# Local attention layers: turning the softmax weights in the two row halves of the array, with the odd heads' token halves of v swapped

## The chip, the cores and the metric

One core of a Trainium2 chip runs the whole program. The metric is the device time of one execution in microseconds (us). The engines are named as in the profile: PE (TensorE, with its weight loads as PEld), DVE (VectorE), ACT (ScalarE), POOL (GpSimd) and SP (the queue that issues DMAs).

## The reference

The program computes four residual blocks over x of shape (8, 512, 256), each followed by a layer norm: a 16-head attention with a gate, a slot attention with 16 experts, a retention block, and two local attention layers. The change touches the last block alone. Cut to what matters, one of its two layers is

```
h = shift_token(x); q, k, v = split(h @ wqkv)            # 8 heads of 64
q, k = rotary_xpos(l2norm(q) * qs, l2norm(k) * ksc)
# blocks of 128 queries; each looks at its own 128 keys and the 128 before
sim = where((i < j) | (i > j + 128) | (j == -1), -max, q * 8 @ k.T)
o = softmax(sim) @ v
x = x + o @ wo
h = layer_norm(shift_token(x)) @ w1 + b1
x = x + (a * gelu(g)) @ w2 + b2                          # a, g = split(h)
```

The first block of each sequence has no keys before it (the mask j == -1).

## The kernel before

All engines follow orders written out by hand and meet at semaphores (`wait_ge`, `then_inc`); `Fresh.wait_ge` (L40) leaves out waits already seen. Blocks 1 to 3 of the program end at about 1000 us; what follows is `Block4`.

**Slots.** Block 4 works on 64 tiles (2 layers x 8 sequences x 4 blocks of 128 tokens). `tensor4`, `scalar4`, `vector4` and `gpsimd4` (L1872, L2082, L2188, L2388) walk through slots n = 1, 2, ... and in each treat four tiles at different stages: a = n (projection), b = n - 1 (turning q and k, scores, exp), c = n - 2 (dividing by the sums, turning the weights), d = n - 3 (attend, output projection, adding to x). The MLP of a sequence is spread in pieces over four parts of each slot (`mlp_pieces`, L1786), and repeats every four slots.

PE's order in a slot is: queries' projection (L1932), turn q (L1958), keys' projection, turn k, MLP part 1, attend d (L2011 for a tile that opens a sequence, L2017 and L2022 for others), scores b (L1976), values a (L1946), MLP part 2, turn half of c's weights (L1991), output projection d (L2033), turn the other half, MLP parts 3 and 4. In the MLP, L2073 and L2077 are the gate and lin products, L2051 the product down, L2059 and L2064 turn x and the normalised rows.

**Turning the weights.** The softmax weights of a head have queries on partitions, but attend needs keys there. `tensor4_weights` (L1980) turns them by 128x128 blocks with the identity as the moving operand: per pair of heads 2 heads x 2 windows (the keys before, the own keys), or 2 x 1 for an opening tile. Each pair fills one bank. DVE copies the banks of pairs 0 and 2 (`vector4_weights`, L2305, L2311), ACT those of 1 and 3 (`scalar4_weights`, L2158, L2164). The divided weights stand in `probs[i % 2]`, where max, exp and divide also work.

**Attend.** `tensor4_attend` (L1994) runs in four quadrants of the array: a 64-row half of the keys by a 64-column head. Sums over the two row halves go to banks 5 and 2; because of the mask, half of each window's block is zero and is left out. ACT copies bank 2 (L2105), DVE adds bank 5 (`vector4_sums`, L2266, L2269). An opening tile uses all 128 rows and bank 5 alone, and DVE copies it (L2274).

**The ring of banks.** Banks 3, 4, 6, 7 are a ring (`Ring`, L60). The list of its uses in `layout4` (L1823) follows PE's order: q, k, part 1's pieces, the four score banks, part 2's pieces, the four banks of turned weights, parts 3 and 4. Before PE writes a bank, `emptied4` (L1859) waits until the use four places earlier has been emptied: scores by DVE's max (L2258), q by ACT (`scalar4_queries`, L2130, L2134), k by DVE's copy (L2202), a gate by ACT's GELU (L2184), a lin by DVE (L2351), back and hT by DVE and ACT (L2343, L2175, L2347, L2179), down by DVE (L2334).

**DVE, ACT, POOL.** DVE in a slot: divide c (L2240, L2244), copy k, squared lengths a (L2281), MLP part 1, sums d, max b, MLP part 2, copy weights 0, rotate a's queries (L2292, L2295), add d to x (L2225), copy weights 2, rotate a's keys, MLP part 3, scale a (`vector4_scale`, L2303), MLP part 4. In slots with n mod 4 = 3, part 4 also takes row statistics (L2616, L2619), and part 1 of the slot after ends with a normalise of four operations (L2631). ACT: divide c (L2127), copy q, squares a (L2141), MLP part 1, copy bank 2, copy values (L2147), exp b, first half (L2155), MLP part 2, copy weights 1, exp second half, copy weights 3, parts 3 and 4. POOL: `gpsimd4_tile` (L2398) takes the power -1/2 of the lengths (L2407) and adds the halves of the rotation (L2411); `gpsimd4_mlp` copies rows and adds a bias (L2431, L2439).

```
for group in range(2):
    for hh in range(2):
        self.emptied4(w, "s", i, 2 * group + hh)
```

is how scores take two banks at a time.

## Time and profile before

| | us |
|---|---|
| three runs | 2330.47, 2332.06, 2335.05 (median 2332.06) |
| the profiled execution | 2333.25 |
| its span, first to last instruction | 2331.4 |
| mean granted clock of PE | 0.989 |

In the rows, a line of the timeline is: start in us from the span's start, length in us, engine, line of the kernel, operation, operands, count, and in brackets the idle time before it with what ended it. A matmul's end is modelled and overlaps the next one's start, so starts are read. The compiler makes two MATMUL instructions of each f32 product and one of each turned block, and the counts are counts of instructions.

### The profile page before, as it was taken

The page shows a single profiled execution, that of the slowest core. Times are in us where ns is not written, and L with a number is a line of the kernel's source. Part 1 is how long each engine was busy: PE and PEld are TensorE (multiplying, and loading weights), DVE is VectorE, ACT ScalarE, POOL GpSimd, SP SyncE. Part 2 cuts the span into 40 slices and gives each one's busy share as a digit, 9 for nine tenths or more (in the row PEclk, how much of TensorE's full clock was granted, in tenths as well). Part 3 has the DMA queues.
Part 4 walks back from the last instruction along what each step waited for, and adds up shares of the span by engine and source line. Part 5 has one row for each costly group of instructions (what it writes and reads, how often), then busy time and mean ns, then how long its engine had stood idle before and what let it go on. Part 6 is the DMA issues. An engine that isn't in the chain of part 4 may idle for free.

```text
span 2331.4 us, 42446 instructions
## 1 busy us (share of the span) xinstructions
PE 2239.6 (96%) x16257; PEld 1316.2 (56%) x16306; DVE 1635.1 (70%) x4252; ACT 1254.6 (54%) x2823; POOL 732.4 (31%) x730
## 2 busy tenths in 40 slices
PE   7999999999998999989899999999999999999998
PEld 3333333334634867756566666666666666666665
DVE  6788888886502746668777677677767777787763
ACT  4666666665222622247666656665665665566640
POOL 3344323321111411144433233333333333333321
PEclk7999999999998999999999999999999999999999
DMA  7454343333397020010000000000001000000001
GB/s 240 151 158 121 117 119 122 112 91 109 157 422 297 2 91 19 28 39 3 5 6 6 5 2 6 6 2 32 15 6 53 6 15 24 19 6 24 22 23 40
DMA packets 68617, 158.44 MB, mean 68 GB/s; under 512 B 6256, under 2 KB 49120, under 8 KB 63936
## 3 DMA queue, kind: packets, MB, share of 16 engines
q1 hardware_dynamic: 65856, 146.55, 17.8%
q0 software_dynamic: 2560, 9.18, 1.7%
q8 instruction: 130, 2.13, 0.4%
q14 instruction: 71, 0.58, 0.1%
HBM read 116.39 MB, written 35.13 MB: 65 GB/s over the span
## 4 chain that ended last, share of the span: by engine, by line
PE 73%; DVE 14%; DMA 4%; ACT 4%; issue 3%; POOL 1%; SPq 0%; another core or an unknown queue 0%; POOLq 0%; DVEq 0%; ACTq 0%
PE banks L2073 10%; PE banks L2051 7%; PE banks L1932 6%; PE banks L1946 5%; PE banks L232 4%; PE banks L274 4%; PE banks L2033 3%; PE banks L245 3%; PE banks L1976 3%; PE banks L1991 3%; DMA arena<-in_e_W 3%; DVE arena L483 2%; PE banks L1455 2%; PE banks L1958 2%; PE banks L300 2%
## 5 line engine op out<-in xcount | busy, mean ns | idle before, releaser
L483 DVE TENSOR_REDUCE arena<-banks 128x1 f32<-128x512 f32 x512 | 322.6, 681 | 61.2 <-PE banks L232 60.4
L395 ACT ACTIVATE arena<-banks 128x512 f32<-128x512 f32 x512 | 280.3, 596 | 136.1 <-PE banks L245 112.4
L2073 PE MATMUL banks<-arena 128*128 128x512 f32 x640 | 293.2, 594 | 1.0 <-DVE arena L2258 1.0
L2155 ACT ACTIVATE arena<-arena 128x256 f32<-128x256 f32 (+1 forms) x512 | 286.5, 562 | 5.0 <-DVE arena L2264 4.5
L2411 POOL TENSOR_TENSOR arena<-arena 128x512 f32<-128x512 f32 x128 | 162.8, 1272 | 379.8 <-DVE arena L2295 379.8
L1932 PE MATMUL banks<-arena 128*128 128x512 f32 x512 | 241.5, 594 | 2.8 <-DVE arena L2295 2.8
L232 PE MATMUL banks<-arena 96*128 96x512 bf16 x512 | 202.9, 400 | 14.6 <-DVE arena L483 8.9
L2407 POOL TENSOR_TENSOR arena<-arena 128x16 f32<-128x16 f32 x64 | 189.4, 2959 | 5.4
L2127 ACT ACTIVATE arena<-arena 128x256 f32<-128x256 f32 (+1 forms) x256 | 102.1, 471 | 162.9 <-DVE arena L2240 162.9
L2073 PEld LDWEIGHTS banks<-arena 128*128 128x128 f32 x640 | 115.5, 190 | 126.7 <-issue 116.5
L245 PE MATMUL banks<-arena 128*128 128x512 bf16 x463 | 174.6, 382 | 3.1 <-ACT arena L395 2.2
L2051 PE MATMUL banks<-arena 128*128 128x256 f32 x768 | 171.1, 379 | 1.9 <-DVE arena L2351 1.9
L2258 DVE CUSTOM_DVE_ANT_0 arena<-banks,arena 128x256 f32<-128x256 f32 (+1 forms) x512 | 168.7, 386 | 3.5 <-PE banks L1976 3.5
L2051 PEld LDWEIGHTS banks<-arena 128*128 128x128 f32 x768 | 144.5, 190 | 28.0 <-issue 6.2
L232 PEld LDWEIGHTS banks<-arena 96*128 96x128 bf16 x512 | 50.0, 98 | 181.5 <-DVE arena L483 110.9
L1932 PEld LDWEIGHTS banks<-arena 128*128 128x128 f32 x512 | 91.5, 190 | 86.9 <-issue 81.3
L274 PE MATMUL banks<-arena 128*32 128x512 f32 x1024 | 136.4, 605 | 2.5 <-ACT arena L395 1.6
L2147 ACT ACTIVATE arena<-banks 128x512 f32<-128x512 f32 x64 | 38.2, 597 | 180.4 <-PE banks L1946 180.4
L2303 DVE TENSOR_TENSOR arena<-arena 128x512 f32<-128x512 f32 x64 | 81.9, 1279 | 73.6 <-POOL arena L2411 73.6
L1946 PE MATMUL banks<-arena 128*128 128x512 f32 x256 | 126.7, 617 | 0.3 <-ACT arena L2105 0.3
L2033 PE MATMUL banks<-arena 128*128 128x256 f32 x512 | 121.2, 380 | 0.0
L1991 PE MATMUL banks<-arena 128*128 128x128 f32 x896 | 119.8, 272 | 0.5 <-DVE arena L2258 0.3
(304 smaller groups left out, 4225.7 us busy)
## 6 DMA issues: line engine op xcount, KB each, us to landing
arena<-in_e_W SPq DMA_DIRECT2D x16, 2048.0 KB, 15.6
arena<-stacks SPq DMA_DIRECT2D x64, 384.0 KB, 4.7
arena<-in_e_Wg SPq DMA_DIRECT2D x8, 2048.0 KB, 17.6
stacks<-arena SPq DMA_DIRECT2D x32, 384.0 KB, 2.5
stacks<-arena SPq DMA_DIRECT2D x32, 256.0 KB, 2.8
arena<-dens POOLq DMA_DIRECT2D x32, 256.0 KB, 4.8
arena<-in_xT SPq DMA_DIRECT2D x8, 512.0 KB, 7.8
stacks<-arena SPq DMA_DIRECT2D x32, 128.0 KB, 2.6
```

Source lines behind the costliest of these rows:

```text
L232: e.matmul(self.psum[:, k % 3], stack[0:STACK, 0, j, t * P:(t + 1) * P], stack[0:STACK, 1, j, :], start=True, stop=True).then_inc(s["a_max ...
L245: e.matmul(self.psum[:, self.exp_bank1(k)], stack[:, 1, j, t * P:(t + 1) * P], stack[:, 0, j, :], start=True, stop=True).then_inc(s["a_exp ...
L274: i = e.matmul(bank[32 * j:32 * j + 32, :], v[:, t, at:at + 32], ex[:, j], start=t == 0, stop=t == TILES - 1, skip_group_check=True)
L395: e.activation(ex[:, j], self.psum[:, self.exp_bank1(k)], ACT.Exp).then_inc(s["a_e"], 1)
L483: e.tensor_reduce(split(self.maxima[n % 2][:, 0:16], TILES, UNIT)[:, t, j:j + 1], self.psum[:, k % 3], AX.X, ALU.max, negate=True).then_in ...
L1932: k = e.matmul(self.psum[:, side], self.xT[:, b, c, at:at + P], self.wqkv4[:, c, side], start=c == 0, stop=c == 1)
L1946: k = e.matmul(self.psum[:, 2], self.xT[:, b, c, at:at + P], self.wqkv4[:, c, 2], start=c == 0, stop=c == 1)
L1991: k = e.transpose(bank[:, hh, n], pr[:, 2 * pair + hh, n * P:(n + 1) * P], self.ident)
L2033: k = e.matmul(self.psum[:, 2, 0:CH], self.o4[0][:, pair * P:(pair + 1) * P], self.wo4[:, pair], start=pair == 0, stop=pair == 3)
L2051: i = e.matmul(bank[:, t % 2 * CH:(t % 2 + 1) * CH], self.hidden[k][:, at:at + P], self.w2[:, k + t // 2 if last else k], start=k == 0, st ...
L2073: i = e.matmul(bank, weights[:, c], self.hT[:, c], start=c == 0, stop=c == 1)
L2155: k = e.activation(pr[:, h, at:], pr[:, h, at:], ACT.Exp, bias=mx[:, h:h + 1], scale=rn[:, h:h + 1], accum_out=den[:, h:h + 1])
```

## The change

- The turning of c's weights moves from parts 2 and 3 to just after MLP part 1, ahead of attend, on PE; the copies of the turned weights move on ACT and DVE to just after their MLP part 1, ahead of bank 2's copy and of the sums. The ring's list of uses moves with it.
- `probs[0]` now holds scores and exps of every tile; the divide writes into `probs[1]` in another arrangement (`probs4`), where each head pair's eight half windows lie such that three 128-column pairs of half blocks hold what the mask leaves. Turning takes, per head pair, three pairs of instructions, one in each 64-row half of the array, each with 128 weight columns and 64 moving columns, into two banks (two pairs for an opening tile). A `couple` is two head pairs, and waits for both of its banks.
- The copies take 384 columns per bank instead of 512, DVE the banks of the first row half, ACT those of the second. `pT` becomes two sets, used in turn.
- Odd heads thus find their keys in swapped 64-token halves. So `tensor4_values` makes their values from `swapped`, a copy of the tokens with halves exchanged, made by POOL (`gpsimd4_swap`, four copies of 128x64 per tile, ahead of the tile's other POOL work), in four products of 256 columns instead of two of 512.
- `tensor4_attend` reads the new arrangement; an opening tile now also runs in quadrants, so ACT's copy of bank 2 and DVE's add are done for all tiles.

The core of the diff:

```diff
-        self.pT = [split(r.take(512), 2, 2, P) for _ in range(4)]
+        self.pT = [[split(r.take(768), 2, 2, 192) for _ in range(2)] for _ in range(2)]
+        self.swapped = [split(r.take(256), CHUNKS, P) for _ in range(2)]
...
+                if part == 1 and 0 <= c < TILES4:
+                    uses += [("w", c, index) for index in range(4)]
                 if part == 1 and 0 <= b < TILES4:
                     uses += [("s", b, index) for index in range(4)]
-                if part == 2 and 0 <= c < TILES4:
-                    uses += [("w", c, index) for index in range(4)]
...
     def tensor4(self, e, w):
...
+            if c is not None:
+                self.tensor4_weights(e, w, c, 0)
+                self.tensor4_weights(e, w, c, 1)
             if d is not None:
                 self.tensor4_attend(e, w, d)
...
-                self.tensor4_weights(e, w, c, 0)
-                self.tensor4_weights(e, w, c, 1)
             if d is not None:
                 self.tensor4_out(e, w, d)
-            if c is not None:
-                self.tensor4_weights(e, w, c, 2)
-                self.tensor4_weights(e, w, c, 3)
...
     def tensor4_values(self, e, w, i):
...
-        if i >= 3 and (i - 3) % TILES:
-            w.wait_ge("t_oa", halves_before(i - 3) + 1)
-        for c in range(CHUNKS):
-            at = 1 - c + t * P
-            k = e.matmul(self.psum[:, 2], self.xT[:, b, c, at:at + P], self.wqkv4[:, c, 2], start=c == 0, stop=c == 1)
+        if i >= 3:
+            w.wait_ge("t_oa", i - 2)
+        w.wait_ge("t_swap", i + 1)
+        out = split(self.psum[:, 2], PAIRS, 2, HD4)
+        for hh in range(2):
+            for c in range(CHUNKS):
+                at = 1 - c + t * P
+                tokens = self.swapped[i % 2][:, c] if hh else self.xT[:, b, c, at:at + P]
+                k = e.matmul(out[:, :, hh], tokens, split(self.wqkv4[:, c, 2], PAIRS, 2, HD4)[:, :, hh], start=c == 0, stop=c == 1, skip_group_check=True)
...
-    def tensor4_weights(self, e, w, i, pair):
-        windows = (0, 1) if i % TILES else (1,)
-        bank = split(self.bank4("w", i, pair), 2, 2, P)
-        pr = split(self.probs[i % 2][:, 0:2048], H4, 2 * P)
-        if pair % 2:
-            w.wait_ge("t_pna", 2 * i + pair // 2 + 1)
-        else:
-            w.wait_ge("t_pn", 2 * i + pair // 2 + 1)
-        self.emptied4(w, "w", i, pair)
-        for hh in range(2):
-            for n in windows:
-                k = e.transpose(bank[:, hh, n], pr[:, 2 * pair + hh, n * P:(n + 1) * P], self.ident)
-        k.then_inc(self.s["t_pT"], 1)
+    def probs4(self, i, h):
+
+        pair, hh = divmod(h, 2)
+        raw = split(self.probs[0][:, 0:2048], H4, 2, 2, 64)[:, h]
+        view = split(self.probs[1][:, 512 * pair:512 * pair + 512], 2, 4, 64)
+        view = view[:, :, 1:3] if hh else view[:, :, 0::3]
+        return (raw, view) if i % TILES else (raw[:, 1:], view[:, 1:])
+
+    def tensor4_weights(self, e, w, i, couple):
+        banks = [self.bank4("w", i, 2 * couple + half) for half in range(2)]
+        w.wait_ge("t_pn", 2 * i + couple + 1)
+        w.wait_ge("t_pna", 2 * i + couple + 1)
+        self.emptied4(w, "w", i, 2 * couple)
+        self.emptied4(w, "w", i, 2 * couple + 1)
+        places = [(0, 0, 1), (1, 1, 2), (2, 2, 3)] if i % TILES else [(3, 1, 0), (2, 2, 1)]
+        for n in range(2):
+            for place in places:
+                last = n == 1 and place == places[-1]
+                for half in range(2):
+                    if i % TILES:
+                        source, to = place[0] + half, place[0]
+                    else:
+                        source, to = place[0], place[1 + half]
+                    rows, at = slice(64 * half, 64 * half + 64), 512 * (2 * couple + n) + P * source
+                    k = e.transpose(banks[half][:, 192 * n + 64 * to:192 * n + 64 * to + 64], self.probs[1][rows, at:at + P], self.ident[rows, rows])
+                    if last:
+                        k.then_inc(self.s["t_pT"], 1)
...
     def tensor4_attend(self, e, w, i):
...
+            outer, inner = split(pT, 3, 2, 64)[:, 1:3, 0], split(pT, 3, 2, 64)[:, 0:2, 1]
+            for hh in range(2):
+                cols = slice((2 * pair + hh) * HD4, (2 * pair + hh + 1) * HD4)
+                for half in range(2):
+                    rows = slice(64 * half, 64 * half + 64)
+                    near = half == hh
+                    v = own if near or i % TILES == 0 else ahead
+                    k = e.matmul(self.psum[64 * hh:64 * hh + 64, 2 if half else 5, pair * P:(pair + 1) * P], v[rows, cols], outer[rows] if near else inner[rows],
+                                 start=True, stop=i % TILES == 0, skip_group_check=True)
...
     def scalar4(self, e, w):
...
+            self.scalar4_mlp(e, w, n, 1)
+            if c is not None:
+                self.scalar4_weights(e, w, c, 0)
+                self.scalar4_weights(e, w, c, 1)
+            if n == 2:
                 self.scalar3_turn(e, w, SEQS - 1, 0)
-            self.scalar4_mlp(e, w, n, 1)
-            if d is not None and d % TILES:
+            if d is not None:
...
-                self.scalar4_weights(e, w, c, 1)
             if b is not None:
                 self.scalar4_exp(e, w, b, 1)
-            if c is not None:
-                self.scalar4_weights(e, w, c, 3)
...
     def scalar4_divide(self, e, w, i):
...
+        if i:
+            w.wait_ge("t_pT", 4 * i)
         for pair in (1, 3):
             for h in (2 * pair, 2 * pair + 1):
-                k = e.activation(pr[:, h, at:], pr[:, h, at:], ACT.Copy, scale=rden[:, h:h + 1])
+                raw, turned = self.probs4(i, h)
+                k = e.activation(turned, raw, ACT.Copy, scale=rden[:, h:h + 1])
...
     def vector4(self, e, w):
...
             self.vector4_mlp(e, w, n, 1)
+            if c is not None:
+                self.vector4_weights(e, w, c, 0)
+                self.vector4_weights(e, w, c, 1)
             if d is not None:
                 self.vector4_sums(e, w, d)
...
-                self.vector4_weights(e, w, c, 0)
...
-                self.vector4_weights(e, w, c, 2)
...
     def vector4_max(self, e, w, i, half):
...
+        pr, mx = split(self.probs[0][:, 0:2048], H4, 2 * P), self.probs[i % 2][:, 2048:2056]
+        if i:
+            w.wait_ge("t_pn", 2 * i)
+            w.wait_ge("t_pna", 2 * i)
...
     def vector4_sums(self, e, w, i):
...
-        if i % TILES:
-            w.wait_ge("t_oa", halves_before(i) + 1)
-            k = e.tensor_tensor(self.o4[0], self.o4[0], self.psum[:, 5], ALU.add)
-        else:
-            w.wait_ge("t_av", i + 1)
-            if i:
-                w.wait_ge("t_wo", i)
-            k = e.tensor_copy(self.o4[0], self.psum[:, 5])
-        k.then_inc(self.s["t_o"], 1)
+        w.wait_ge("t_oa", i + 1)
+        e.tensor_tensor(self.o4[0], self.o4[0], self.psum[:, 5], ALU.add).then_inc(self.s["t_o"], 1)
...
     def vector4_weights(self, e, w, i, couple):
...
+        to, bank = self.pT[i % 2][couple][:, :, 0], split(self.bank4("w", i, 2 * couple)[:, 0:384], 2, 192)
+        at = 0 if i % TILES else 64
+        w.wait_ge("t_pT", 4 * i + 2 * couple + 1)
+        if i >= 2:
+            w.wait_ge("t_av", i - 1)
+        e.tensor_copy(to[:, :, at:], bank[:, :, at:]).then_inc(self.s["t_pTd"], 1)
...
     def gpsimd4(self, e, w):
...
+                self.gpsimd4_swap(e, w, n)
                 self.gpsimd4_tile(e, w, n)
             self.gpsimd4_mlp(e, w, n)
+
+    def gpsimd4_swap(self, e, w, n):
+        l, b, t = n // LAYER, n // TILES % SEQS, n % TILES
+        if l:
+            w.wait_ge("m_yTd", b + 1)
+            w.wait_ge("m_yTa", b + 1)
+        else:
+            w.wait_ge("r_xTb", b + 1)
+            w.wait_ge("r_xTa", b + 1)
+        if n >= 2:
+            w.wait_ge("t_v", n - 1)
+        for c in range(CHUNKS):
+            at = 1 - c + t * P
+            e.tensor_copy(self.swapped[n % 2][:, c, 0:64], self.xT[:, b, c, at + 64:at + P])
+            k = e.tensor_copy(self.swapped[n % 2][:, c, 64:P], self.xT[:, b, c, at:at + 64])
+        k.then_inc(self.s["t_swap"], 1)
```

## Rows read from the trace of the kernel before

**Rows 1.** The page, part 1: PE's busy time, share of the span, instructions.

```profile
PE 2239.6 (96%) x16257; PEld 1316.2 (56%) x16306; DVE 1635.1 (70%) x4252; ACT 1254.6 (54%) x2823; POOL 732.4 (31%) x730
```

**Rows 2.** Windows: stretch, length, busy time of each engine, granted clock, DMA.

```profile
1000.00:1170.00 170.00, 150.82 (x1368) 98.11 (x1362) 133.33 (x430) 105.56 (x282) 75.58 (x68) 0.99 0.05 16
...
1200.00:2220.00 1020.00, 1017.85 (x7920) 668.51 (x7921) 750.81 (x2237) 616.89 (x1516) 359.66 (x278) 1.00 0.05 14
...
1653.06:1671.27 18.21, 18.21 (x114) 11.10 (x112) 13.28 (x40) 12.99 (x31) 6.10 (x6) 1.00 0.05 14
1671.27:1693.00 21.73, 21.56 (x185) 15.22 (x184) 19.33 (x54) 10.87 (x28) 9.63 (x8) 1.00 0.00 1
...
1713.70:1733.08 19.38, 19.38 (x158) 11.66 (x157) 12.32 (x40) 13.21 (x32) 5.72 (x4) 1.00 0.01 3
sum 80.02, PE 79.85 PEld 52.53 DVE 57.32 ACT 48.47 POOL 27.32; mean PE 19.96 PEld 13.13 DVE 14.33 ACT 12.12 POOL 6.83
```

**Rows 3.** Timeline of PE in slot A: a turned group and what follows.

```profile
1664.35 1.04 PE L1991 MATMUL banks<-arena 128*128 128x128 f32 x8
1665.23 1.89 PE L2033 MATMUL banks<-arena 128*128 128x256 f32 x8
```

**Rows 4.** Groups by line and form: turning, its loads, and ordinary loads.

```profile
L1991 PE MATMUL banks<-arena 128*128 128x128 f32 x896 | 119.8, 272 | 0.5 <-DVE arena L2258 0.3
...
L2051 PEld LDWEIGHTS banks<-arena 128*128 128x128 f32 x768 | 144.5, 190 | 28.0 <-issue 6.2 <-DVE arena L2351 3.5
...
L1991 PEld LDWEIGHTS banks<-arena 128*128 128x128 f32 x896 | 105.0, 140 | 23.3 <-issue 15.3
```

**Rows 5.** Timeline of PE in block 2: four row tiles, 32 moving columns.

```profile
743.70 1.99 PE L990 MATMUL banks<-arena 32*128 32x32 f32 x64 [0.60 <-DVE arena L1217]
```

**Rows 6.** Timeline of PE in slot A: attend, scores, values.

```profile
1658.38 1.04 PE L2011 MATMUL banks<-arena 128*64 128x128 f32 x16
1659.35 1.53 PE L1976 MATMUL banks<-arena 64*64 64x192 f32 x32
1660.81 1.98 PE L1946 MATMUL banks<-arena 128*128 128x512 f32 x4
```

**Rows 7.** Timeline of PE in slot D: attend's start, scores, values.

```profile
1719.82 0.45 PE L2017 MATMUL banks<-arena 64*64 64x128 f32 x8
...
1721.21 1.48 PE L1976 MATMUL banks<-arena 64*64 64x192 f32 x32
1722.62 1.98 PE L1946 MATMUL banks<-arena 128*128 128x512 f32 x4
```

**Rows 8.** DVE's scale multiply, all 64: shortest, median, longest in ns.

```profile
L2303 DVE TENSOR_TENSOR arena<-arena x64: 687/693/2832, 1021.6 to 2226.8; 128x512 f32<-128x512 f32 x64
```

**Rows 9.** Timeline of ACT in A, B and D: gate 5, queries' copy, gate 2.

```profile
1658.60 0.47 ACT L2184 ACTIVATE arena<-banks,arena 128x256 f32<-128x256 f32 x1 [0.64 <-PE banks L2077]
...
1676.27 0.57 ACT L2134 ACTIVATE arena<-banks 128x512 f32<-128x512 f32 x1
...
1719.93 0.69 ACT L2184 ACTIVATE arena<-banks,arena 128x512 f32<-128x512 f32 x1 [1.56 <-PE banks L2073]
```

**Rows 10.** Timeline of DVE from A's end into B: scale, lin 5, normalise.

```profile
1670.93 1.21 DVE L2303 TENSOR_TENSOR arena<-arena 128x512 f32<-128x512 f32 x1 [0.43 <-POOL arena L2411]
...
1678.55 0.48 DVE L2351 SCALAR_TENSOR_TENSOR arena<-banks,arena 128x256 f32<-128x256 f32 x1
1678.94 1.37 DVE L2631 TENSOR_SCALAR arena<-arena 128x256 f32<-128x256 f32 x4
```

**Rows 11.** Timeline of PE in slot B: scores' second half, values.

```profile
1679.08 0.88 PE L1976 MATMUL banks<-arena 64*64 64x192 f32 x16 [0.17 <-DVE arena L2351]
1679.89 1.98 PE L1946 MATMUL banks<-arena 128*128 128x512 f32 x4
```

**Rows 12.** Timeline of DVE in slot C: the keys' copy.

```profile
1697.52 0.69 DVE L2202 COPY arena<-banks 128x512 f32<-128x512 f32 x1 [1.94 <-PE banks L1958]
```

**Rows 13.** Timeline of PE in slot C: scores, values.

```profile
1698.80 1.06 PE L1976 MATMUL banks<-arena 64*64 64x64 f32 x32
1699.79 1.98 PE L1946 MATMUL banks<-arena 128*128 128x512 f32 x4
```

More of the change, by code:

```diff
@@ L1994, in tensor4_attend @@
     def tensor4_attend(self, e, w, i):
-        first = i % TILES == 0
-        w.wait_ge("t_vn", i + 1)
+        w.wait_ge("t_vn", min(i + 3, TILES4))
         if i:
             w.wait_ge("t_o", i)
-        if not first:
             w.wait_ge("t_x", i)
+        own, ahead = self.vn[i % 4], self.vn[(i - 1) % 4]
         for pair in range(PAIRS):
-            if pair % 2:
-                w.wait_ge("t_pTa", 2 * i + pair // 2 + 1)
-            else:
-                w.wait_ge("t_pTd", 2 * i + pair // 2 + 1)
-            heads = [slice((2 * pair + hh) * HD4, (2 * pair + hh + 1) * HD4) for hh in range(2)]
-            if first:
-                for hh in range(2):
-                    k = e.matmul(self.psum[64 * hh:64 * hh + 64, 5, pair * P:(pair + 1) * P], self.vn[i % 4][:, heads[hh]], self.pT[pair][:, hh, 1],
-                                 start=True, stop=True, skip_group_check=True)
+            w.wait_ge("t_pTd", 2 * i + pair // 2 + 1)
+            w.wait_ge("t_pTa", 2 * i + pair // 2 + 1)
+            pT = self.pT[i % 2][pair // 2][:, pair % 2].rearrange("p a b -> p (a b)")
+            outer, inner = split(pT, 3, 2, 64)[:, 1:3, 0], split(pT, 3, 2, 64)[:, 0:2, 1]
[7 more added lines that the diff above has]
+                                 start=True, stop=i % TILES == 0, skip_group_check=True)
+            if i % TILES == 0:
@@ L2013, in tensor4_attend @@
                 continue
             for hh in range(2):
-                for half, (bank, n) in enumerate(((5, 1), (2, 0))):
+                cols = slice((2 * pair + hh) * HD4, (2 * pair + hh + 1) * HD4)
+                for half in range(2):
                     rows = slice(64 * half, 64 * half + 64)
-                    k = e.matmul(self.psum[64 * hh:64 * hh + 64, bank, pair * P:(pair + 1) * P], self.vn[(i - 1 + n) % 4][rows, heads[hh]], self.pT[pair][rows, hh, n],
-                                 start=True, stop=False, skip_group_check=True)
@@ L2019, in tensor4_attend @@
-            for hh in range(2):
-                for half, (bank, n) in enumerate(((5, 0), (2, 1))):
-                    rows, some = slice(64 * half, 64 * half + 64), slice(64 * half, 64 * half + 64)
-                    k = e.matmul(self.psum[64 * hh:64 * hh + 64, bank, pair * P + 64 * half:pair * P + 64 * half + 64], self.vn[(i - 1 + n) % 4][rows, heads[hh]],
-                                 self.pT[pair][rows, hh, n, some], start=False, stop=True, skip_group_check=True)
+                    near = half == hh
@@ L2024, in tensor4_attend @@
+                    at = 0 if near else 64
+                    k = e.matmul(self.psum[64 * hh:64 * hh + 64, 2 if half else 5, pair * P + at:pair * P + at + 64], (ahead if near else own)[rows, cols],
+                                 pT[rows, 0:64] if near else pT[rows, 320:384], start=False, stop=True, skip_group_check=True)
         k.then_inc(self.s["t_av"], 1)
@@ L2156, in scalar4_exp, with scalar4_weights @@
         k.then_inc(self.s["t_exp"], 1)
-    def scalar4_weights(self, e, w, i, pair):
-        b4 = split(self.bank4("w", i, pair), 2, 2, P)
-        at = 0 if i % TILES else 1
-        w.wait_ge("t_pT", 4 * i + pair + 1)
-        if i:
-            w.wait_ge("t_av", i)
-        e.activation(self.pT[pair][:, :, at:], b4[:, :, at:], ACT.Copy).then_inc(self.s["t_pTa"], 1)
+    def scalar4_weights(self, e, w, i, couple):
+        to, bank = self.pT[i % 2][couple][:, :, 1], split(self.bank4("w", i, 2 * couple + 1)[:, 0:384], 2, 192)
+        end = 192 if i % TILES else P
+        w.wait_ge("t_pT", 4 * i + 2 * couple + 2)
+        if i >= 2:
+            w.wait_ge("t_av", i - 1)
+        e.activation(to[:, :, 0:end], bank[:, :, 0:end], ACT.Copy).then_inc(self.s["t_pTa"], 1)
     def scalar4_mlp(self, e, w, slot, part):
@@ L2235, in vector4_divide @@
     def vector4_divide(self, e, w, i):
-        at = 0 if i % TILES else P
-        pr, extra = split(self.probs[i % 2][:, 0:2048], H4, 2 * P), self.probs[i % 2][:, 2048:]
+        extra = self.probs[i % 2][:, 2048:]
         den, rden = extra[:, 8:16], extra[:, 16:24]
```

33 lines of the change are left out of this document (11 added, 22 removed).

## The prediction, made before any run of the changed kernel

> **What bounds the kernel now.** I read the page first, then windows, then one engine at a time. The page's busy times [rows 1] only say that TensorE (PE) is the fullest engine over the whole span; the windows say where. From 1200 to 2220 us, inside the local layers, PE is busy 1017.85 of 1020 us at a granted clock of 1.00, and a group of four slots, one sequence, takes 80.02 us [rows 2]. So there is nothing to win there by shortening a wait: PE's own work has to shrink, and any wait that PE is given costs its full length. I call the four slots by what stands in them: A is 1653.06 to 1671.27 (its attended tile opens a sequence; gate 5 in part 1), B 1671.27 to 1693.00 (lin 5), C 1693.00 to 1713.70 (nothing of the MLP in part 1; its scored tile opens a sequence), D 1713.70 to 1733.08 (gate 2; its turned tile opens a sequence). From slot 10 to slot 65 each kind stands 14 times with all its pieces. Within a slot I give times from its start.
>
> **What is taken away.** Eight turned blocks of 128x128 take 0.88 us of PE, from the first of them to the first of the output projection [rows 3]; a tile has two such groups, an opening tile one, 896 instructions in all [rows 4]. That is 1.76 us in A, B and C and 0.88 in D. Taken alone, 14 x 6.16 is 86 us.
>
> **What is put in their place.** A tile now has 24 instructions in 12 pairs (an opening tile 8 pairs), each pair reading the two row halves into two banks, 64 columns wide. Streaming: 128 columns take 0.11 us [rows 3], so 64 take 0.055. Loading: nothing in the trace turns a half block, so I bound the pair. From below 0.055, both halves wholly side by side. From above 0.115, the pace of the groups of four row-tiled instructions with 128-column weights and only 32 columns to stream, where the load must be what sets it: 64 instructions in 1.99 us, so (1.99 - 0.27) / 15 [rows 5]. I take 0.06, near the lower end: the load of a turned block lasts 140 ns where the ordinary load of the same 128x128 shape lasts 190 [rows 4], so turning loads faster, and the upper end comes from ordinary loads. Halves one after the other would be 2 x 0.055, the same as the upper end. So six pairs are 0.36 us, four 0.24.
>
> The Trainium skill (TensorE: Matmul & The Clock Gate, LDWEIGHTS) says that a weight load costs its columns at 1.2 GHz, whatever the rows: an estimate of 0.107 us for each pair's 128 columns. By that page the pairs are the upper end and the whole is some 17 us longer than by my value. The load rows of this trace speak against it for turned blocks, since at one shape they differ by 50 ns.
>
> **The modes.** Going from whole-array or column-halved work into quadrants leaves a gap. In A, sixteen column-halved matmuls start at 1658.38, two side by side in each 0.11 us, 0.87 in all; the first quadrant matmul starts at 1659.35, 0.97 later [rows 6]. The row-halved turning now stands right before attend, so one more such gap of 0.10 is paid per slot; bounds 0 and 0.20, I take 0.10 (0.14 in A with a slower first group).
>
> **Values, attend, swap, first-tile sums.** Values go from two 512-column products to four of 256 columns, with the same columns streamed; nothing, since PE alone sets them and a 190 ns load hides under 256 columns. Attend has the same quadrant streams: 1.39 us in D [rows 7]; the opening tile's two half-array streams per 0.11 us become four quadrants with half the rows, again 0.9. The swap, four 128x64 copies on POOL, lies early in a slot, long before values; it stands in POOL's queue ahead of the norms' tile work, where POOL was idle. ACT's extra 128x512 copy in A ends before values need it. What the swap can cost is DVE: the scale multiply takes 693 ns in the median and up to 2832 beside POOL work [rows 8]. With the swap beside it I expect some 0.5 us later DVE in D of the second layer, where the length squares end just before gate 2's GELU: five slots, 2.5 us.
>
> **The waits that come in.** This is the term that decides. The four turned banks come from the ring of four right after part 1. Each bank must be emptied of the use four places earlier: for the last turned bank of a tile this is part 1's MLP piece, just made, and in C, which has none, it is the keys' bank. The turning of heads 4 to 7 waits for that, and behind it in PE's queue stand attend, scores, values and everything later.
> - A: gate 5's GELU ends at 6.01 [rows 9]; turning 4 to 7 can start at 6.06. Add 0.36, then entry and attend 1.03, then scores 1.41: values at 8.86 instead of 7.75 [rows 6]. 1.11 later, 1.76 removed: -0.65.
> - B: heads 0 to 3 wait for ACT's queries copy, which ends 5.57 [rows 9]. Then lin 5: today it ends 1679.03, or 7.76 [rows 10], and PE already feels it: the second half of the scores waits 0.17 us for L2351 [rows 11]. All of DVE's beginning of B hangs on the scale multiply, which starts 0.34 us before A's end [rows 10]. In new A, PE's part after MLP part 2 loses 1.76 of 6.92 us and DVE's part to the scale only two copies and a short wait, 1.3 of 6.58, so the scale starts some 0.4 later in the slot, and lin 5 ends 8.16. Turning at 8.20; + 0.36 + 1.49 + 1.41: values at 11.46 instead of 8.62 [rows 11]. 2.84 - 1.76 = +1.08. DVE's copies of the turned weights come behind a normalise of 1.37 us [rows 10]; two copies, each under the 0.69 of a 512-column one, are out at 10.0 and 10.5, just as the score halves ask (10.05 and 10.75).
> - C: keys' copy ends 5.20 [rows 12]; turning at 5.25; + 0.36 + 1.49 + 0.99: values at 8.09 instead of 6.78 [rows 13]. 1.31 - 1.76 = -0.45.
> - D: gate 2's GELU ends 6.92 [rows 9]; turning at 6.97; + 0.24 + 1.49 + 1.41: 10.11 instead of 8.92 [rows 7]. 1.19 - 0.88 = +0.31.
> After values, each slot runs on as now. The sum is +0.29 us per sequence, 14 times: +4 us. Slots 2 to 9 leave PE idle for 19 of 170 us [rows 2]: they run through DVE and POOL, where copies that go from between the rotations come back ahead of the sums, and the swap is added. I take 0, between -5 and +5. With 2.5 for the swap: +6.6 on the profiled execution's 2333.25 us, 2339.9. That execution is 1.2 us over the median of the three runs, so for the median I say 2339. About 0.2% (4.7 us) is what a measurement can tell from no change, so this is slower by a little more than that.
>
> **The rivals.**
> 1. The load sets the turning (0.115 a pair). Then six pairs after each wait in A, B, C and four in D cost 0.055 x 22 = 1.2 us more per sequence: +17, 2356. For: the only row-tiled 128-column rows [rows 5]. Against: the shorter load of turned blocks [rows 4].
> 2. Lin 5's bank is free early, on the other side: faster. If DVE and ACT come to B no later than to C (keys and lengths are then done by about 6.4, lin 5 by 6.9), B turns at 6.9 instead of 8.2: -1.3 us 14 times, -18, 2321. It decides from 7.9: below that the sequence total turns negative. For: DVE's idle time elsewhere in the sequence. Against: at the start of B DVE has scale, statistics, lin 3 and divide in one unbroken row, until 7.76 today.
> 3. The waits bind, but less: no extra entry and no shift of DVE, -0.8 us per sequence, 11 us less than my sum, and no swap cost, 2.5 less: 2326 for all of it, 2332 for half. Mostly no measurable change.
> 4. The turning's saving is real and no bank is in the way, 2333 - 14 x 3.2 = 2288. It needs banks that the ring's arithmetic doesn't give; 3 in 100.
>
> **How the numbers follow.** My forecast's own case, 2335 to 2346: 0.42, nearly all slower, a quarter within 0.2%. Rival 1: 0.18, slower. Rival 2: 0.12. Rival 3: 0.25, of which a third falls below 2327.4. Rival 4: 0.03. Together: faster 0.23, same 0.27, slower 0.50. The range of 8 in 10 reaches from 2321, rival 2, to 2360, rival 1 with the swap's contention doubled.
>
> **What would show it.** Right: the turned groups' PE time near 0.36 us per six pairs; new idle time of PE before them, of about 0.25 us in A, 2.3 in B (mostly for DVE's lin 5, today's L2351), 0.4 in C and 0.5 in D (ACT's GELU), some 48 us in all; slots of about 17.6, 22.8, 20.3 and 19.7 us. PE busy share down to about 96% in the steady stretch, clock still 1.00. Wrong: pairs at 0.11 us; B's turning starting before 7.9; scores waiting for the weights' copies (then the price lies behind attend, and more is lost); values waiting for POOL's swap; or slots of 16 to 20 us with PE full, which would be rival 4.

## The result and the profile after

| | before | changed |
|---|---|---|
| runs on one chip, median (us) | 2333.56 (4) | 2373.61 (4: 2370.63 to 2381.97) |
| profiled execution, its span | 2333.25, 2331.4 | 2381.97, 2380.2 |
| mean granted clock | 0.989 | 0.977 |

The ratio is 1.0178, 95% interval 1.0147 to 1.0209: slower by 1.8%, as forecast in sign and far off in size. The predicted 2339 and even the range's end at 2360 are too low. The profiled execution is the slowest of the four, 8.4 us above the median, so sums taken from its trace are a little larger than those of the median run. The page of the changed kernel, part 1, then windows: the two stretches of [rows 2], and four slots, C, D, A and B in this order. `L1926` is the projection, `L2002` the turning, `L2025` and `L2035` attend, `L1974` scores, `L1944` values, `L2046` the output projection.

```profile
PE 2234.8 (94%) x17330; PEld 1347.1 (57%) x17330; DVE 1621.1 (68%) x4252; ACT 1256.2 (53%) x2839; POOL 802.3 (34%) x986
```

```profile
1000.00:1170.00 170.00, 139.81 (x1377) 99.65 (x1376) 123.14 (x399) 93.91 (x257) 82.29 (x106) 0.93 0.05 16
1200.00:2220.00 1020.00, 978.84 (x8500) 672.88 (x8491) 720.18 (x2177) 600.49 (x1490) 406.34 (x474) 0.98 0.04 13
...
1642.24:1662.65 20.41, 20.05 (x185) 14.58 (x184) 11.87 (x40) 11.10 (x29) 7.35 (x10) 1.00 0.00 1
1662.65:1682.50 19.85, 19.38 (x169) 12.23 (x168) 12.60 (x40) 13.01 (x32) 7.20 (x10) 1.00 0.09 28
1682.50:1700.22 17.72, 17.57 (x142) 11.06 (x141) 12.51 (x39) 13.93 (x32) 6.75 (x8) 1.00 0.05 16
1700.22:1723.13 22.91, 20.73 (x198) 15.38 (x197) 19.24 (x54) 10.56 (x29) 10.67 (x13) 1.00 0.01 1
```

PE was full in [rows 2]; now it lacks 41 us of 1020, and the stretch's clock is 0.98. The four slots are 17.7, 22.9, 20.4 and 19.85 us, within 0.15 of the 17.6, 22.8, 20.3 and 19.7 foretold. So the slots' model held here, and the error must be elsewhere. PE's waits in the steady stretch (columns: us in all, times, longest) are the foretold ones too, 39.6 us in twelve and a half sequences, for which 3.45 each, 43, were expected:

```profile
PE banks L2002 <- DVE arena L2362: 20.8, 13, 1.6
PE banks L2002 <- ACT arena L2150: 7.6, 13, 0.6
PE banks L2002 <- ACT arena L2200: 6.9, 16, 0.6
PE banks L2002 <- DVE arena L2218: 4.3, 12, 0.4
```

PE's timeline in that B slot, and DVE's ahead of the wait:

```profile
1706.29 0.59 PE L2002 MATMUL banks<-arena 64*128 64x64 f32 x12 [0.58 <-ACT arena L2150]
1708.47 0.59 PE L2002 MATMUL banks<-arena 64*128 64x64 f32 x12 [1.60 <-DVE arena L2362]
1708.99 0.45 PE L2025 MATMUL banks<-arena 64*64 64x128 f32 x8
...
1710.38 1.48 PE L1974 MATMUL banks<-arena 64*64 64x192 f32 x32
1711.79 1.99 PE L1944 MATMUL banks<-arena 128*128 128x256 f32 x8
```

```profile
1706.66 1.28 DVE L2292 TENSOR_REDUCE arena<-arena 128x8 f32<-128x512 f32 x2 [0.96 <-ACT arena L2157]
1707.85 0.47 DVE L2362 SCALAR_TENSOR_TENSOR arena<-banks,arena 128x256 f32<-128x256 f32 x1
```

Lin 5 ends 8.10 into the slot (8.16 foretold), the second couple starts at 8.25 (8.20), values at 11.57 (11.46). Attend takes 1.39 us. In the next B slot (it starts at 1781.09) the waits are the same, but attend takes 2.61 and the scores 1.78:

```profile
1789.35 0.59 PE L2002 MATMUL banks<-arena 64*128 64x64 f32 x12 [1.60 <-DVE arena L2362]
1789.87 0.71 PE L2025 MATMUL banks<-arena 64*64 64x128 f32 x8
...
1792.48 1.85 PE L1974 MATMUL banks<-arena 64*64 64x192 f32 x32
1794.26 1.99 PE L1944 MATMUL banks<-arena 128*128 128x256 f32 x8
```

Windows from attend's start to the start of values in that slot, and from the second couple's start into values in the B slot above:

```profile
1789.81:1794.30 4.49, 4.49 (x102) 3.93 (x97) 2.51 (x7) 1.09 (x2) 2.50 (x1) 0.62 0.02 4
...
1708.46:1713.39 4.93, 4.92 (x115) 4.37 (x116) 4.19 (x16) 1.09 (x2) 2.97 (x1) 1.00 0.01 3
```

The granted clock is 0.62 in the one and 1.00 in the other: part of the stretch went at the lower level, 1.2 GHz. Ten of thirteen B slots were longer than 22.91, nine of them by 1.3 us or more, and in these nine the granted clock fell. The tenth, from 1372.92, is 0.76 longer at a granted clock of 1.00 (4.95 us from its second couple on): attend takes 1.39 there, and the time is lost inside the scores, where PE pauses without a releaser:

```profile
1384.79 0.54 PE L1974 MATMUL banks<-arena 64*64 64x192 f32 x2 [0.23 <-issue]
```

**Where 48.8 us of span went.** I summed slot lengths, from one first projection to the next, in both traces; up to slot 61 there are 13 of each kind.

| stretch | changed minus before | foretold |
|---|---|---|
| before the first slot (unchanged code) | +4.7 | 0 |
| slots 0 to 9 | +13.6 | 0, at most 5 |
| 13 A | -6.4 | -8.5 |
| 13 B | +29.7, of it 14.6 above 22.91 each | +14.0 |
| 13 C | -3.4 | -5.9 |
| 13 D | +6.9 | +4.0, and 2.5 for the swap |
| from slot 62 on | +3.6 | 0.3 |

Two sums are missing from the forecast: some 14 us for the clock (13.8 of the 14.6, in nine slots; 0.8 is the tenth), 13.6 for the early slots. The 4.7 ahead of the first slot is not the change's: the twelve other kernels run for this document begin their first slot between 997.7 and 1005.4 us, this one at 1005.5, the kernel before at 1000.8. In the early slots PE waits mostly for ScalarE's copies of the queries (`L2150`) and of the values (`L2163`) and for the divide (1000 to 1170 us):

```profile
PE banks L2002 <- ACT arena L2150: 6.5, 8, 0.8
PE banks L2002 <- DVE arena L2261: 6.0, 6, 2.4
PE banks L2046 <- ACT arena L2163: 5.0, 7, 0.8
PE banks L1974 <- ACT arena L2180: 3.1, 1, 3.1
```

`L2261` is the divide, which the turning now meets in the first part of a slot; `L2180` is ScalarE's copy of turned weights, for which the scores wait. Neither of these two waits stands in these slots before. Part of the 13.6 is the clock again: keep_busy_two below runs the same code in slots 0 to 7 and takes 124.3 us for them at a mean clock of 0.97, the changed kernel 126.7 at 0.95, the kernel before 115.6 at 1.00.

### The profile page after: what moved, and what is told of

Read it like the earlier page. It is cut to its first block, busy times and chain, and to the rows that moved or that the text cites. A ratio compares the mean times of both kernels' runs of the same rounds, so it can differ in the third digit from the quotient of the medians.

```text
span 2380.2 us, 45019 instructions
## 1 busy us (share of the span) xinstructions
PE 2234.8 (94%) x17330; PEld 1347.1 (57%) x17330; DVE 1621.1 (68%) x4252; ACT 1256.2 (53%) x2839; POOL 802.3 (34%) x986
## 4 chain that ended last, share of the span: by engine, by line
PE 70%; DVE 13%; ACT 8%; issue 4%; DMA 3%; POOL 2%; SPq 0%; POOLq 0%; DVEq 0%; ACTq 0%
PE banks L2086 7%; PE banks L2064 7%; PE banks L1944 5%; PE banks L1926 5%; PE banks L232 4%; PE banks L274 4%; PE banks L245 4%; PE banks L1974 3%; PE banks L2025 3%; PE banks L2046 3%; PE banks L1455 2%; DVE arena L483 2%; ACT arena L2143 2%; PE banks L300 2%; PE banks L2002 2%
## 5 line engine op out<-in xcount | busy, mean ns | idle before, releaser
L2086 PE MATMUL banks<-arena 128*128 128x512 f32 x640 | 292.6, 593 | 0.8 <-DVE arena L2276 0.8
L1926 PE MATMUL banks<-arena 128*128 128x512 f32 x512 | 240.9, 593 | 0.3 <-DVE arena L2306 0.3
L245 PE MATMUL banks<-arena 128*128 128x512 bf16 x512 | 193.4, 384 | 2.9 <-ACT arena L395 2.2
L2064 PE MATMUL banks<-arena 128*128 128x256 f32 x768 | 171.1, 379 | 1.9 <-DVE arena L2362 1.9
L1926 PEld LDWEIGHTS banks<-arena 128*128 128x128 f32 x512 | 91.8, 190 | 82.7 <-issue 80.8
L2002 PE MATMUL banks<-arena 64*128 64x64 f32 x1408 | 73.4, 235 | 60.3 <-DVE arena L2362 20.8
L1944 PE MATMUL banks<-arena 128*128 128x256 f32 x512 | 128.4, 394 | 0.3 <-issue 0.3
L2163 ACT ACTIVATE arena<-banks 128x512 f32<-128x512 f32 x64 | 38.2, 597 | 167.9 <-PE banks L1944 167.9
L2046 PE MATMUL banks<-arena 128*128 128x256 f32 x512 | 121.5, 380 | 5.0 <-ACT arena L2163 5.0
## 6 DMA issues: line engine op xcount, KB each, us to landing
arena<-in_e_Wg SPq DMA_DIRECT2D x8, 2048.0 KB, 17.7
```

The lines of the kernel that those rows point to most:

```text
L245: e.matmul(self.psum[:, self.exp_bank1(k)], stack[:, 1, j, t * P:(t + 1) * P], stack[:, 0, j, :], start=True, stop=True).then_inc(s["a_exp ...
L1926: k = e.matmul(self.psum[:, side], self.xT[:, b, c, at:at + P], self.wqkv4[:, c, side], start=c == 0, stop=c == 1)
L1944: k = e.matmul(out[:, :, hh], tokens, split(self.wqkv4[:, c, 2], PAIRS, 2, HD4)[:, :, hh], start=c == 0, stop=c == 1, skip_group_check=True)
L2046: k = e.matmul(self.psum[:, 2, 0:CH], self.o4[0][:, pair * P:(pair + 1) * P], self.wo4[:, pair], start=pair == 0, stop=pair == 3)
L2064: i = e.matmul(bank[:, t % 2 * CH:(t % 2 + 1) * CH], self.hidden[k][:, at:at + P], self.w2[:, k + t // 2 if last else k], start=k == 0, st ...
L2086: i = e.matmul(bank, weights[:, c], self.hT[:, c], start=c == 0, stop=c == 1)
```

## The experiments

Medians, with the ratio to runs of the kernel before on the same chip. Edits are against the changed kernel unless another is named.

**keep_busy and keep_busy_two: is it the clock?** Between the two couples of a B slot, work that is thrown away (eight products in keep_busy, two in keep_busy_two; two waits are left out here):

```diff
                 self.tensor4_weights(e, w, c, 0)
+                if (n - MLP_FIRST) % MLP_STEP == 1 and n >= 8 and a is not None:
...
+                    for k in range(8):
+                        e.matmul(self.psum[:, 5], self.ident, self.wqkv4[:, 0, 2], start=True, stop=True, skip_group_check=True)
                 self.tensor4_weights(e, w, c, 1)
```

> The changed kernel with eight matmuls of 512 columns, about 0.21 us each, put into TensorE's wait for lin 5 in every B slot (they write a bank that attend overwrites), so the wait of 2.1 us is filled and nothing else is moved. Theory (the granted clock): after the wait the clock falls to the lower level and attend and the scores stream at half pace, 1.6 us in 10 of 13 B slots, some 15 us. Filled, attend takes 1.39 us in every B slot, B is 22.9 to 23.1 us throughout, the granted clock of the steady stretch is 1.00, and the time is 2356 to 2363 instead of 2373.6. Rival (operands): attend is longer since its operands, or the turned banks' copies, come late after the wait; then it still takes 2.6 us and the time stays at 2370 to 2378.

Measured: 2434.28 us (1.0434). I had sized the filler wrongly: a written f32 matmul of 512 columns is two instructions of 0.44 us, so eight filled 7.1 us and every B slot became 28.3 long. That is 22.9 + 5.4, the distance by which the second couple moved (8.25 to 13.65): all thirteen alike, no slot with a slow attend. So I sized it again.

> As keep_busy with two written matmuls instead of eight: each becomes two instructions of 0.44 us, so eight filled 7.1 us and pushed the second couple from 8.25 to 13.65; two fill 1.76 us of the wait and end at 8.2 to 8.35. Theory (the granted clock): every B slot takes 22.9 to 23.0 us as those of the changed kernel where the clock held, the clock of the steady stretch is 1.00, and the time is 10 to 16 us under the changed kernel's 2373.6, so 2357 to 2364. Rival: the B slots of 24.4 us are longer for another reason (late operands of attend); they stay, and the time is above 2370.

Measured: 2363.82 us (2362.07 to 2366.2; ratio 1.0135, 1.0121 to 1.0149, against 1.0178). B is 23.16 in the median and never above 23.4; the clock of the steady stretch is back:

```profile
1200.00:2220.00 1020.00, 999.39 (x8670) 677.70 (x8669) 724.29 (x2187) 603.33 (x1498) 408.93 (x476) 1.00 0.04 13
```

Adding 1.76 us of useless work to each B slot made the kernel about 10 us faster; in the traces the thirteen B slots are 11.1 us shorter together. The operands' rival falls: nothing about them changed. (The expectation's ten slots are nine, as said above.)

**lin_first and lin_first_norm_ahead: is it lin 5's bank?** VectorE's order alone, in B slots, in outline:

```diff
-    self.vector4_lengths(e, w, a)
     ... lin 5 ...
+    self.vector4_lengths(e, w, a)
-    ... normalise ...          # stays here in lin_first_norm_ahead
     self.vector4_weights(e, w, c, 0)
     self.vector4_weights(e, w, c, 1)
+    ... normalise ...
```

> The changed kernel with VectorE's order in B slots changed: lin 5 ahead of the squared lengths (it then fits between the keys' copy, done at 5.5, and the squares, 6.4), and the normalise behind the copies of the turned weights. Theory (lin 5's bank is the wait that decides): the bank is free at 6.1 instead of 8.2, the second couple follows the first at 6.45, attend starts at 6.9, values at 9.7; B takes 21.0 to 21.3 us instead of 22.9 to 24.5, the clock holds. 14 times 1.8, and 15 for the clock: 2331 to 2337. Rival 1 (the mechanism is not lin 5 but the late queries' copy or the copies of the turned weights): B stays above 22.3, the time above 2360. Rival 2: the late normalise makes VectorE late for the output sums; then idle time appears ahead of the output projection in B and the time lies between, 2340 to 2355.

Measured: 2347.4 us (2339.93 to 2350.63; ratio 1.0057, 1.0044 to 1.0071). B is 21.10 in seven of thirteen slots, as foretold. PE and VectorE in such a slot (from 1605.81):

```profile
1611.88 0.97 PE L2002 MATMUL banks<-arena 64*128 64x64 f32 x24 [0.59 <-ACT arena L2150]
1612.78 0.45 PE L2025 MATMUL banks<-arena 64*64 64x128 f32 x8
...
1615.58 2.00 PE L1944 MATMUL banks<-arena 128*128 128x256 f32 x8
```

```profile
1611.35 0.48 DVE L2366 SCALAR_TENSOR_TENSOR arena<-banks,arena 128x256 f32<-128x256 f32 x1
1612.25 1.28 DVE L2296 TENSOR_REDUCE arena<-arena 128x8 f32<-128x512 f32 x2 [0.42 <-ACT arena L2157]
```

Lin 5 fits into a hole in which VectorE waits for the squares anyhow; both couples run as one group and the 1.60 us wait is gone. The deciding term is shown. The time is 10 us above the expectation. In the profiled executions the thirteen B slots are 32.5 us shorter together where I had 40: six of them are still up to 1.4 longer than 21.1 (5.6 us), at a clock of 1.00, with gaps inside the scores for which the profile has no releaser (2.8 us in four), of the kind seen above at 1384.79. The DMA's records hint at what they are. Queue q8, of the kind "instruction", brings 139 packets of 16 KB in a run, 64 bytes for each of PE's 35,548 instructions. The four gaps end at 1535.7, 1694.9, 1854.2 and 2012.1, 1.4 to 1.6 us after a packet of q8 has landed (1534.1, 1693.5, 1852.7, 2010.7), and the one at 1384.79 ends 1.5 us after one. So PE probably waited for its own instructions; no run tests it. Slots 0 to 9 are as long as before this edit (167.4).

> As lin_first, but the normalise of 1.37 us stays ahead of the copies of the turned weights. The second couple starts at 6.45 as there, attend at 6.9 to 8.3. Theory: what is late next is the scores' first bank, emptied only by VectorE's copy at about 9.7, so the scores start at 9.75 instead of 8.3 and values at 11.2; B is 22.5 us. 14 times 0.4 less than the changed kernel, and the clock's 15 us only where a wait of 1.4 us leaves it alone: 2350 to 2368. Rival: the scores don't wait for these copies; then the time is that of lin_first.

Measured: 2355.43 us (1.0093), B 22.32 throughout, the clock at 1.00. The next wait is where it was expected:

```profile
1612.19 1.53 PE L1974 MATMUL banks<-arena 64*64 64x192 f32 x32 [1.00 <-DVE arena L2323]
```

The scores' bank is emptied by VectorE's copy behind the normalise. In the changed kernel the 1.60 us wait hid that.

**old_place and twice: what the half blocks save, and what a change of mode costs.** In old_place the couples, their banks and copies go back (the part on PE, in outline):

```diff
-    self.tensor4_weights(e, w, c, 0)      # ahead of attend
-    self.tensor4_weights(e, w, c, 1)
...
     self.tensor4_mlp(e, w, n, 2)
+    self.tensor4_weights(e, w, c, 0)
     self.tensor4_out(e, w, d)
+    self.tensor4_weights(e, w, c, 1)
```

> The half-block turning, the swap and the new attend kept, but the turning, its copies and its banks put back where they were: the first couple after part 2 of the MLP, the second after the output projection. Theory (the place is what costs, the half blocks save): no new wait, each couple of six pairs takes 0.37 us and 0.1 to 0.2 for going into row halves, instead of 1.03; three slots of a sequence gain 0.7 to 0.9 us and the opening one 0.2 to 0.3. 14 times 2.3 to 3.0, so 32 to 42 us less than before: 2292 to 2302. Slots 2 to 9 no longer than before. Rival (the half-block scheme itself costs: the swap's contention, ScalarE's longer queue, the quadrant attend): slots 2 to 9 stay 10 us longer than before and the gain is at most 25 us, 2308 or more.

Measured: 2322.74 us (ratio 0.996, 0.9946 to 0.9973), faster than before, with slots 0 to 9 at 153.0 (before 153.8, changed 167.4). The place was what cost. But the gain is about a quarter of what I expected: A, B and C gain 0.26 to 0.31 us and D loses 0.27. PE in a C slot, where nothing waits, of old_place and then of the kernel before:

```profile
1616.32 5.34 PE L2065 MATMUL banks<-arena 128*128 128x256 f32 x24
1621.59 0.59 PE L2003 MATMUL banks<-arena 64*128 64x64 f32 x12
1622.11 1.99 PE L2047 MATMUL banks<-arena 128*128 128x256 f32 x8
1624.04 0.59 PE L2003 MATMUL banks<-arena 64*128 64x64 f32 x12
1624.56 3.70 PE L2087 MATMUL banks<-arena 128*128 128x512 f32 x8
1628.10 0.59 PE L1927 MATMUL banks<-arena 128*128 128x512 f32 x1
```

```profile
1621.59 5.34 PE L2051 MATMUL banks<-arena 128*128 128x256 f32 x24
1626.77 1.04 PE L1991 MATMUL banks<-arena 128*128 128x128 f32 x8
1627.65 1.89 PE L2033 MATMUL banks<-arena 128*128 128x256 f32 x8
1629.38 1.04 PE L1991 MATMUL banks<-arena 128*128 128x128 f32 x8
1630.26 3.60 PE L2073 MATMUL banks<-arena 128*128 128x512 f32 x8
1633.69 0.59 PE L1932 MATMUL banks<-arena 128*128 128x512 f32 x1
```

From start to start, before: 5.18, 0.88, 1.73, 0.88, 3.43; now 5.27, 0.52, 1.93, 0.52, 3.54. Each group is 0.36 shorter, and what lies around the two groups is 0.40 longer in all: 0.1 for each way into the row halves and 0.1 for each way out. 0.32 of the 0.72 is left. D loses because an opening tile's one group of 0.88 becomes two, of 0.25 for four pairs and 0.35 besides each by the next run: 1.20.

twice issues every half-block turn of old_place two times, into the same place.

> old_place with every half block turned twice into the same place, so that each group has twelve pairs (eight in D) instead of six (four). Theory (a pair costs 0.062 us, and 0.16 us of each group belongs to the change of mode): A, B, C longer by 12 x 0.062 = 0.74 us, D by 0.50, and the groups 0.90 and 0.78 us long instead of 0.53 and 0.47. 2355 to 2363. Rival (the load of 128 columns sets the pace at 0.115 once a group is longer than the buffers): 1.4 us in A, B, C and 0.9 in D, 2385 to 2400.

Measured: one run of 2369.56 us (before, on that chip, 2337.34), A 18.64 where old_place has 17.90, B 22.22 for 21.47, D 20.14 for 19.64:

```profile
1622.20 0.96 PE L2003 MATMUL banks<-arena 64*128 64x64 f32 x24
1623.10 1.99 PE L2047 MATMUL banks<-arena 128*128 128x256 f32 x8
1625.02 0.96 PE L2003 MATMUL banks<-arena 64*128 64x64 f32 x24
1625.91 0.66 PE L2078 MATMUL banks<-arena 128*128 128x128 f32 x4
```

Six more pairs cost 0.90 - 0.52 = 0.38, 0.062 a pair, the slots' 0.74 and 0.50. So of a group's 0.52 six pairs are 0.37 and 0.15 comes once. With the 0.20 around it, a group costs 0.35 besides its pairs. The total lies 7 us above its expectation; I read the slots, not the one time.

**after_out and between: other places.** after_out is old_place with both couples behind `tensor4_out`.

> old_place with both couples of the turning behind the output projection. Theory: in old_place each couple costs 0.15 us of gap beyond its six pairs, and the projection between them 0.19 more; together there is one such group less, so each slot is 0.25 to 0.35 us shorter, 56 slots: 2304 to 2309. Rival: the gap belongs to the pairs themselves (a first one always costs more) and not to the change of mode; then nothing is gained, 2320 to 2325.

Measured: 2351.31 us (1.0082). Neither theory: the MLP's next bank is one that the group has just filled, so PE waits 0.27 us behind it for the first copy, and VectorE's copies, now later, push all of its row back, until in B the scores wait 1.30 us for lin 5. A, C and D are as long as in old_place, within 0.01 us, so what one group less would give without that wait stays open:

```profile
1609.97 0.88 PE L1974 MATMUL banks<-arena 64*64 64x192 f32 x16 [1.30 <-DVE arena L2364]
...
1617.86 0.66 PE L2077 MATMUL banks<-arena 128*128 128x128 f32 x4 [0.27 <-DVE arena L2324]
```

between is lin_first with the two couples behind `tensor4_attend`, and ScalarE's copy of attend's bank ahead of its weights' copies.

> lin_first with the turning behind attend instead of ahead of it, so that attend (1.1 to 1.4 us) covers the wait for the ring's bank, and with ScalarE's copy of attend's second bank ahead of its copies of the turned weights. Theory (the ring's wait, not the half-block scheme, is what the change paid for; next to attend the row halves cost at most one more change of mode): no wait for lin 5 or a GELU; A 17.3 us, C 19.8, D 19.1 to 19.2; in B the scores' first bank waits for VectorE's copy, 0 to 0.6 us, 20.9 to 21.4. That is 2.4 to 3.1 us per sequence under before: 2290 to 2301. Rival: the scores now wait for the turned weights' copies in every slot (0.3 to 0.7 each): 2308 or more.

Measured: 2335.62 us (11 runs; ratio 1.0009, 0.9999 to 1.0019). A 17.91, B 21.03, C 20.40, D 19.82. B is as expected, the rest falls to the rival: the scores wait for VectorE's copy in 43 slots of the steady stretch and for ScalarE's in 8, some 50 in all. Slots 0 to 9 are as long as in the changed kernel (168.0), another 14 us over the kernel before.

```profile
1608.78 1.53 PE L1974 MATMUL banks<-arena 64*64 64x192 f32 x32 [0.37 <-DVE arena L2326]
```

**no_swap: the swap.** The call of `gpsimd4_swap` and its wait go; odd heads' values take unswapped tokens, so that part of the output is another.

> The changed kernel without the swapped copies of the tokens on GpSimd: the odd heads' values take the tokens in their old order (this part of the output is another one); the four 256-column products stay. Theory (the swap costs little in the steady stretch, where it ran early in a slot): A, B, C unchanged, D of the second layer 0 to 0.25 us shorter, slots 2 to 9 shorter by 0 to 5 us of the 13.5 that they gained: 2366 to 2373. Rival (the swap's shared port with VectorE is behind the longer slots 2 to 9): these come down by 8 us or more, below 2365.

Measured: 2378.55 us (1.0196, 1.0182 to 1.021), not faster at all. A, C and D are the same to 0.01 us, D of the second layer too (19.15), and slots 0 to 9 are 167.4. The swap costs nothing.

**move_only and start_old: the early slots.** move_only is the kernel before with its whole-block turning ahead of attend and a second buffer. start_old is the changed kernel with the old places while `n < 10`.

> The kernel before with its whole-block turning moved ahead of attend (a second buffer for the turned weights, the copies moved with it, nothing of the half blocks or the swap). Theory (order and ring banks make the waits, whatever the turning costs): only the last of the four banks needs part 1's piece, and 1.3 us of turning of the first three covers A, C and most of D, so A, C stay at 18.2 and 20.7, D 19.4 to 19.6; B waits 1.4 to 1.5 us for lin 5, 23.1 to 23.3 and 1.6 more where the clock falls; slots 2 to 9 lengthen by 10 to 16 us as in the changed kernel, since the turning now stands between the divide and attend. 2366 to 2386. Rival (slots 2 to 9 lengthen through the half-block scheme, its ScalarE copies or the single buffer of scores): they stay within 3 us of before, and the time is 2352 to 2370.

> The changed kernel with the turning, its copies and banks at their old places in slots 2 to 9 alone. Theory: the 13.5 us that slots 0 to 9 gained come from the order, a loop of scores, largest values, exponentials, divide and turning that now has to close within a slot; at the old places it goes: 2358 to 2363, slots 0 to 9 152 to 156 us. Rival: the half-block scheme; they keep 160 us or more, and the time is above 2366.

Measured: move_only 2375.77 us (1.0166), B 22.95, C 20.7, D 19.8, A 18.5 (0.3 more than I gave it; I did not follow that up), slots 0 to 9 164.8; start_old 2365.92 us (1.0129, 1.0112 to 1.0146, with before at 2337.34 on that chip; its profiled run 2357.33 is its fastest), slots 0 to 9 151.7. Its median is 3 us over the expectation, the slots are as expected. Windows from 1000 to 1170, move_only and then start_old:

```profile
1000.00:1170.00 170.00, 143.78 (x1240) 91.73 (x1241) 126.49 (x403) 99.87 (x268) 72.09 (x65) 0.97 0.05 16
```

```profile
1000.00:1170.00 170.00, 147.32 (x1492) 99.02 (x1491) 131.81 (x427) 108.11 (x293) 89.72 (x114) 1.00 0.05 16
```

11 us of the early slots come with the order alone, without any half block, and all of it goes with the order. The clock there, 0.93 in the changed kernel, is 1.00 again. The old place is what these slots need, and not merely a turning that stands behind attend: they take 168.0 us in between and 162.7 in after_out, where it stands even later than before.

**old_place_lin_first: the version that wins.** Both findings together.

> old_place with lin 5 ahead of the squared lengths on VectorE in B slots. Theory: in old_place the scores of B wait 0.1 to 0.3 us for lin 5, 3.2 us in 12 slots; that wait goes and nothing takes its place, B 21.2 instead of 21.5: 2317 to 2321. Rival: VectorE's later squared lengths make it late elsewhere, B stays at 21.4 or more, 2322 or more.

Measured: 2317.3 us (2315.02 to 2320.53; ratio 0.9919, 0.9905 to 0.9932). B 21.09. It beats both kernels, by 0.8% and, by the two ratios, about 2.5%. How much of the 0.8% the kernel before would gain from the new order on VectorE alone was not run; its B slots wait 0.2 us for lin 5.

## Why the prediction was wrong, point by point

- **What bounds the kernel, what is removed.** Right. Each wait given to PE cost at least its length.
- **The pair, 0.06 us.** Right: 0.062. Rival 1 (0.115) is out. The rule of the Trainium skill (TensorE: Matmul & The Clock Gate, LDWEIGHTS), a load's columns at 1.2 GHz and by estimate 0.107 us a pair, is not what twice shows for turned half blocks.
- **The entry, 0.10.** Mis-sized: a group costs 0.15 once besides its pairs, and 0.10 for each way in and out from whole-array work. Here values start 0.11 to 0.15 later than worked out in every kind of slot, 0.56 us a sequence.
- **"For the last turned bank of a tile this is part 1's MLP piece."** Right, and the term that decides among the slots; lin_first removes it. Rival 2 held its mechanism (below 7.9 the sum turns), but its condition did not occur: lin 5 ended at 8.10.
- **"Clock still 1.00."** The step that failed most. I priced B's wait at its own length. In nine of thirteen slots the granted clock fell around it and attend and scores streamed in part at the lower level, together 13.8 us; with the wait filled they don't. The steady stretch of before could not show it, as PE hardly waited there; I should have kept a rival for it, since the change's own working put two waits, 2.3 us in all, into one slot. The Trainium skill (TensorE: Matmul & The Clock Gate, A second HAM failure mode: psum-queue depth-cycling) tells of another kernel in which short idle times between groups of matmuls bring the clock down and up again; these rows agree.
- **"I take 0, between -5 and +5" for slots 2 to 9.** The second failed step, +13.6. Without MLP pieces those slots run through a loop: scores, largest values, exponentials, divide, turning, and behind it in PE's queue attend and the next scores. I looked at VectorE's copies and not at what PE's queue holds behind a turning that now comes first. That the order is the cause is shown (move_only, start_old); that it acts through this loop is my reading of the waits, and after_out, with its turning late and 162.7 us, says that the loop alone is not the whole account.
- **The swap, 2.5 us.** Wrong, 0. D of the second layer did lose 0.65 instead of 0.47, but without the swap as well: gate 2's GELU ends at 7.07 there, behind a later queue on ScalarE.

Range and chances: of the forecast's 0.50 for slower, none reached 2360; 2373.6 is about its 2339, 14 for the clock, 14 for the early slots and some 7 in small terms, the 0.56 a sequence above all.

## What to carry to other kernels

On a full engine, ask of each moved step which buffer it takes and who emptied that buffer last; the saving is worth nothing in a place where the ring's last user has just begun. Here a wait on PE of 1.6 us cost nearly as much again in the work behind it, so fill it, or order the emptying engine so that it never arises. Small matmuls in another tile shape are cheap by the pair and dear by the group: count the changes of shape before counting columns.

## What the hardware showed that I had not expected

Two idle times of 0.58 and 1.60 us, 2.2 us apart, bring the granted clock down in nine slots (to 0.62 over 4.5 us in the one shown) and leave it at 1.00 in four with the same waits. With the second one filled it is 1.00 in all thirteen. It is also 1.00 in the steady stretch with idle times of 0.58 and 1.00, 3.4 us apart (lin_first_norm_ahead), and with one of 1.30 in each B slot (after_out). A pair of loads of half blocks with 128 columns each, one per row half, runs at 0.062 us, though one such load lasts 143 ns in the records. A group of them costs 0.35 us besides, 0.10 going in, 0.15 within and 0.10 coming out: as much as five and a half pairs.
